# Queries and keys turned by VectorE in 32x32 blocks, in place of TensorE transposes

## What is computed

```python
q = rope(rmsnorm(x @ Wq.T), pos)          # 32 positions x 32 heads x 128
k = rope(rmsnorm(x @ Wk.T), pos)          # 32 positions x  8 heads x 128
v = x @ Wv.T
k_all, v_all = [cached 512 keys, k], [cached 512 values, v]   # pages by block_table
scores = einsum('bqhd,bkhd->bhqk', q, repeat(k_all, 4)) / sqrt(128)
probs  = softmax(where(valid, scores, -1e30))
out    = einsum('bhqk,bkhd->bqhd', probs, repeat(v_all, 4)) @ Wo.T
```

## Time and profile before

| | us |
|---|---|
| median of 3 runs | 3128.94 (3127.9 to 3129.48) |
| the profiled execution | 3137.39 |
| its span | 3135.6 |
| TensorE busy | 3013.1 (96%) |
| VectorE busy | 1545.1 (49%) |
| ScalarE busy | 1285.4 (41%) |
| GpSimd busy | 1467.3 (47%) |

### The profile page before, as it was taken

The page is one execution under the profiler, slowest core; times in us unless marked ns, Lnnn a source line. Parts: engine busy times, 40 slices in busy tenths (PEclk is TensorE's granted clock), DMA queues, the critical chain, the costliest instruction groups (busy, mean ns, idle before and its releaser), DMA issues. The chain is left out here.

```text
span 3135.6 us, 56006 instructions
## 1 busy us (share of the span) xinstructions
PE 3013.1 (96%) x15256; PEld 2016.5 (64%) x15264; DVE 1545.1 (49%) x4043; ACT 1285.4 (41%) x3017; POOL 1467.3 (47%) x1262
## 2 busy tenths in 40 slices
PE   6889999999999999999999999999999998899997
PEld 4566666666666666666666666666666665565664
DVE  4544444444444444444444444444444444576665
ACT  2444444444444444444444444444444442222222
POOL 5465555555555555555555555555555551000000
PEclk9899999999999999999999999999999999899998
DMA  8444443434444444545444444444444344321110
GB/s 302 172 116 120 119 118 118 118 118 118 118 117 118 119 119 119 199 119 172 119 119 119 119 119 119 119 119 119 119 116 118 117 118 135 98 52 44 38 43 14
DMA packets 413898, 368.45 MB, mean 118 GB/s; under 512 B 83415, under 2 KB 347755, under 8 KB 412731
## 3 DMA queue, kind: packets, MB, share of 16 engines
q1 hardware_dynamic: 358490, 186.81, 21.0%
q0 software_dynamic: 48208, 165.16, 17.0%
q10 hardware_dynamic: 7056, 14.46, 1.2%
HBM read 335.13 MB, written 22.71 MB: 114 GB/s over the span
## 5 line engine op out<-in xcount | busy, mean ns | idle before, releaser
L551 DVE CUSTOM_DVE_ANT_0 ps_s<-ps_s,mask 128x544 f32<-128x544 f32 x512 | 374.9, 732 | 912.6 <-PE ps_s L383 738.5
L283 POOL DMA_INDIRECT v_sb<-in_v_rows_w,v_row x504 | 491.9, 976 | 483.5 <-PE ps_oT L408 274.1
L342 PE MATMUL ps_t<-wqkv,xT 128*128 128x512 f32 x1488 | 703.9, 596 | 0.0
L406 PEld LDWEIGHTS ps_oT<-pT,v_sb 128*128 128x128 f32 x4096 | 527.1, 192 | 184.2 <-issue 183.1
L454 ACT ACTIVATE ps_s<-ps_s,nmax 128x544 f32<-128x544 f32 x512 | 352.3, 688 | 596.5 <-DVE nmax L551 546.6
L406 PE MATMUL ps_oT<-pT,v_sb 128*128 128x128 f32 x4096 | 541.4, 275 | 7.8 <-issue 7.8
L366 PE MATMUL ps_t<-wo,oT 128*128 128x512 f32 x1024 | 524.7, 596 | 2.5 <-ACT oT L469 0.9
L382 PE MATMUL ps_s<-k_sb,qT 128*128 128x416 f32 x1024 | 448.5, 520 | 20.3 <-DVE pT_new L567 7.9
L469 ACT ACTIVATE oT<-ps_oT 128x128 f32<-128x128 f32 x512 | 142.3, 278 | 676.1 <-PE ps_oT L408 633.8
L561 DVE TENSOR_SCALAR p_sb<-ps_s,rinv 128x544 f32<-128x544 f32 x512 | 401.4, 784 | 23.5
L391 PEld LDWEIGHTS ps_pT<-ident_sb,p_sb 128*128 128x128 f32 x2048 | 251.5, 141 | 188.7 <-issue 184.3
(11 more groups left out here) (225 smaller groups left out, 3504.1 us busy)
## 6 DMA issues: line engine op xcount, KB each, us to landing
k_sb<-in_kT SPq DMA_DIRECT2D x2048, 64.0 KB
v_sb<-in_v_rows_w,v_row POOLq DMA_INDIRECT x512
v_new<-v_raw SPq DMA_DIRECT2D x128, 64.0 KB, 2.0
wo<-in_wo_w POOLq DMA_DIRECT2D x2, 4096.0 KB, 13.8
y_scratch<-y_sb SPq DMA_DIRECT2D x32, 256.0 KB
xT<-x1T_scratch POOLq DMA_DIRECT2D x31, 256.0 KB, 4.4
wqkv<-in_wqkv_w ACTq DMA_DIRECT2D x6, 1024.0 KB, 25.1
wqkv<-in_wqkv_w POOLq DMA_DIRECT2D x6, 1024.0 KB, 13.2
```

The costliest lines, as they stand in the source:

```text
L283: e.indirect_dma_start(out=v_sb[:, b % 2, c, :], out_offset=None, in_=A["v_rows_w"], in_offset=bass.IndirectOffsetOnAxis(ap=v_row[:, b, c: ...
L342: m = e.matmul(ps_t[bank_of(t)][:, :], xT[:, k, :], wqkv[:, k, 512 * t:512 * t + 512], start=k == 0, stop=k == KC - 1)
L406: e.matmul(ps_oT[:, :], v_sb[:, b % 2, c, h * D:(h + 1) * D], pT[:, u % 2, c, :], start=c == 0, stop=False)
L551: e.tensor_tensor_reduce(out=scores(u), in0=scores(u), in1=mask[:, b % 2, :], scale=-SCALE, scalar=3e38, op0=ALU.add, op1=ALU.min, accum_o ...
```

## The change

TensorE's `turn_q` and ScalarE's `copy_q` are gone from the rounds; the first round's queries and keys are still turned by TensorE, ahead of the rounds. VectorE turns the others, straight from `rot` in SBUF to `qT` and `kT_new` in SBUF, in 32 x 32 blocks: for each sequence b (32 partitions of `rot`) and each quarter j of the 128 numbers, one instruction over the 16 query heads (32 x 512), and one over the four key heads (32 x 4 x 32). That is 32 instructions a round. `qT` is laid out anew, so that what an instruction writes lies together. A table says how many stand in each unit, before and behind the normalisation: units 11 to 15 of the round before, and units 0 to 3 of the round itself, since only the first sequence is needed at once. The waits go by `q_turned`, now counted by instruction. VectorE's loop becomes one over two rounds.

```diff
-    TURN_AT = {8: 0, 9: 1, 10: 2, 11: 3, 12: 4}
+    TURN_AT = {11: (2, 2), 12: (2, 2), 13: (1, 1), 14: (1, 1), 15: (2, 2), 0: (1, 2), 1: (1, 3), 2: (2, 2), 3: (1, 4)}
@@ rotate (GpSimd), before the first write of rot
-            e.wait_ge(W.q_turned, NQT * r)
+            e.wait_ge(W.q_turned, blocks_turned(r - 1, GB - 1) if not (isinstance(r, int) and r == 1) else NQT)
@@ TensorE
-            def turn_q(r, t):
...
-                for h in range(4):
-                    m = e.transpose(ps_t[1][:, h * P:(h + 1) * P], rot[:, 4 * t + h, :], ident[:, :])
-                m.then_inc(q_turned, 1)
@@ score
-                if u == 0:
-                    e.wait_ge(q_copied, NQT * (r + 1))
                 if h == 0:
+                    if first(r):
+                        e.wait_ge(q_copied, NQT)
+                    else:
+                        e.wait_ge(q_turned, blocks_turned(r, b))
@@ ScalarE
-            def copy_q(r, t, i):
...
-                e.activation(to, of, ACT.Copy).then_inc(q_copied, 1)
@@ VectorE
+            def turn(r, i, m):
+                b, j = divmod(m, TURNS)
+                rows, at = slice(S * b, S * b + S), slice(S * (j % 4), S * (j % 4) + S)
+                if m == 0:
+                    e.wait_ge(rope_step, STEPS * (r + 1))
+                    wait(e, scored, UNITS * (r - 1))
+                if j == 4:
+                    e.wait_ge(placed, GB * (r - 1) + b + 1)
+                if j < 4:
+                    e.transpose(qT[at, i, b, :, :], rot[rows, 0:HQH, at]).then_inc(q_turned, 1)
+                else:
+                    e.transpose(kT_new[at, :, rows], rot[rows, HQH:HT, at]).then_inc(q_turned, 1)
...
                     if ahead(r, u, 1) is not None:
                         copy_pT(*ahead(r, u, 1))
+                    turns(r, i, u, 0)
                     if ahead(r, u, 2) is not None:
                         norm(*ahead(r, u, 2))
+                    turns(r, i, u, 1)
...
-            rounds(e, body)
+            pairs(e, body)
```

More of the change, by code:

```diff
@@ L42, with blocks_turned @@
 STEPS, STEPS1 = 15, 6
+TURNS = 2 * (P // S)
+def blocks_turned(r, b):
+    return NQT + TURNS * GB * (r - 1) + TURNS * (b + 1)
 class Shared:
@@ L63, in __init__ @@
         self.w4 = sb("w4", [P, 4, D], F32)
-        self.qT = sb("qT", [P, 2, HKH, GB, REP, S], F32)
+        self.qT = sb("qT", [P, 2, GB, HQH, S], F32)
         self.kT_new = sb("kT_new", [P, HKH, P], F32)
@@ L162, in attention @@
     wo_done, y_copied = sem("wo_done"), sem("y_copied")
-    TURN_AT = {8: 0, 9: 1, 10: 2, 11: 3, 12: 4}
+    TURN_AT = {11: (2, 2), 12: (2, 2), 13: (1, 1), 14: (1, 1), 15: (2, 2), 0: (1, 2), 1: (1, 3), 2: (2, 2), 3: (1, 4)}
+    TURN_NEXT = sum(sum(TURN_AT[u]) for u in range(11, 16))
     OUT_AT = {6: (0, 2), 7: (2, 4), 8: (4, 5), 9: (5, 7), 10: (7, 8), 11: (8, 10), 12: (10, 11), 13: (11, 13), 14: (13, 14), 15: (14, 16)}
@@ L174, in wait @@
             e.wait_ge(s, n)
[L176 to L181, removed]
     def pairs(e, body):
@@ L333, in project @@
                         e.wait_ge(dma_x, 16 * r)
-                        wait(e, q_copied, NQT * r)
+                        e.wait_ge(summed, NQT * r)
                     if t == 1:
@@ L380, in score @@
                 wait(e, p_copied_v, n - 1)
-                q = qT[:, i, h, b, :, :].rearrange("p r s -> p (r s)")
+                q = qT[:, i, b, REP * h:REP * h + REP, :].rearrange("p r s -> p (r s)")
                 e.matmul(ps_s[u % 2][:, FROM:512], q, k_sb[:, b % 2, 0:PAGES1, h, :], start=True, stop=True)
@@ L418, in body @@
                         out_product(r - 1, 1 - i, h0, h0 + 1)
-                    if u in TURN_AT and not last(r):
-                        turn_q(r + 1, TURN_AT[u])
                     if ahead(r, u, 1) is not None:
@@ L475, in copy_y, with place @@
                 e.activation(y_sb[:, :], ps_t[0][:, :], ACT.Copy).then_inc(y_copied, 1)
-            def copy_q(r, t, i):
[L478 to L482, removed]
-                else:
-                    wait(e, placed, GB * r)
-                    to, of = kT_new[:, :, :], ps_t[1][:, :].rearrange("p (h n) -> p h n", h=HKH)
-                e.activation(to, of, ACT.Copy).then_inc(q_copied, 1)
-            def place(r, b):
-                if b == 0:
-                    e.wait_ge(q_copied, NQT * (r + 1))
+            def place(r, b):
+                if first(r):
+                    e.wait_ge(q_copied, NQT)
+                else:
+                    e.wait_ge(q_turned, blocks_turned(r, b))
                 wait(e, scored, UNITS * r + HKH * (b - 1))
@@ L510, in body @@
                         copy_pT(*ahead(r, u, 1))
-                    if u in TURN_AT and not last(r):
-                        copy_q(r + 1, TURN_AT[u], 1 - i)
             exp(0, 0)
@@ L573, in table, with turns, body @@
                 make_tables(e, W, csn[:, 0, :], csn[:, 1, :])
-            def body(r):
+            def turn(r, i, m):
[10 more added lines that the diff above has]
+                    e.transpose(kT_new[at, :, rows], rot[rows, HQH:HT, at]).then_inc(q_turned, 1)
+            def turns(r, i, u, part):
+                if u not in TURN_AT or first(r) and u < 11 or last(r) and u >= 11:
+                    return
+                units = range(11, u) if u >= 11 else range(u)
+                m = (0 if u >= 11 else TURN_NEXT) + sum(sum(TURN_AT[v]) for v in units) + part * TURN_AT[u][0]
+                for n in range(m, m + TURN_AT[u][part]):
+                    turn(r + 1 if u >= 11 else r, 1 - i if u >= 11 else i, n)
+            def body(r, i):
                 for u in range(UNITS):
@@ L896, in copy_q @@
                 if t < HKH:
-                    to, of = W.qT[:, 0, t, :, :, :].rearrange("p b r s -> p r b s"), ps_p[t % 2][:, :].rearrange("p (r b s) -> p r b s", r=REP, b=GB)
+                    to, of = W.qT[:, 0, :, REP * t:REP * t + REP, :].rearrange("p b r s -> p r b s"), ps_p[t % 2][:, :].rearrange("p (r b s) -> p r b s", r=REP, b=GB)
                 else:
```

## The result

| | before | changed |
|---|---|---|
| median of 6 runs, us | 3128.97 (3127.87 to 3129.87) | 3119.32 (3109.05 to 3120.99) |
| profiled execution, us (span) | 3137.4 (3135.6) | 3109.05 (3107.2) |
| ratio of the times | | 0.9961, 95% interval 0.9948 to 0.9975 |

The kernel became faster by 9.7 us. The forecast was 25.7. Of all executions of this case one, of the kernel before with a third buffer, ran at a mean granted clock of 0.87 in place of 0.99 and took 3457.84 us; the ratio in its row leaves it out.

A forecast was written before the change was run, and what follows sets the result against it. TensorE, busy 96% of the span, was taken as the bound; -67.4 for transposes, -7.9 for waits and 31 x 1.6 of new wait gave -25.7 us, from 3128.9 to 3103 us; own range 3085 to 3120, whole range 3062 to 3148.

The forecast's parts named there:

- what TensorE loses: Five groups of transposes leave TensorE's rounds: 2.175 us a round, 67.4 us over 31 rounds.
- what VectorE gains: Turns of 0.73 us (large) and 0.33 us (small) add 17 us a round, bringing VectorE to about 2070 us busy.
- the fullest unit: Unit 11, with four large turns: VectorE's chain makes TensorE's score of unit 13 wait 0.3 us a round.
- the disturbance: Unit 11: TensorE's signals come late during GpSimd's burst of gathers, adding 1.3 us, for 1.6 us of wait a round.
- the burst hangs on GpSimd's rotation: Rotation starts from unit 3's third sum, ahead of removed transposes, so TensorE moves 1.3 to 1.7 us forward against the burst.
- Rival 1: Lateness in unit 11 goes, only 0.3 us of wait a round left: -66 us, 3063 us; chance 0.27.
- Rival 2: Full lateness, 2.6 us a round, and the clock falls after TensorE's holes in 11 rounds: +24 us, 3153 us; chance 0.18.
- Rival 3: Large turn takes two cycles a value, 1.26 us, so unit 11's wait is 3.7 us: +39 us, 3168 us; chance 0.07.
- Rival 4: The wait lands at 2.2 to 2.6 us and eats the gain: within 6 us of 3129; chance 0.13.
- The other edits: GpSimd's wait for the last turn, waits on the turn count and VectorE's loop over two rounds: all counted at nothing.

The follow-up runs named there:

- third buffer: Third buffer for gathered values, the fourth sequence's gathers issued at round start, attention output of 8 heads: on changed kernel 3063.95 us, on kernel before 3115.25 us.
- two gathers away: Two of the fourth sequence's four gathers in own memory, issued at round start, single mask: on changed kernel 3069.16 us, on kernel before 3120.29 us.
- the still later gathers: Kernel before with an unused GpSimd power of 128x12 numbers between rotation and gathers: 3144.36 us, ratio 1.0034.
- the small turns: Changed kernel with VectorE turns of one head in place of 16 or 4 inside the loops: 3109.26 us; with the third buffer too, 3057.55 us.

## Why the prediction was right and wrong

**Right: what TensorE loses.** Units 8 to 11 are shorter by 0.44 us each once nothing else is late, and unit 12 by 0.35 (two gathers away against the kernel before with the same: 2298.0 against 2355.9 us for 30 rounds, 57.9 of the 65.3 us of the term).

**Right: what VectorE gains.** A large turn takes 0.702 us (0.73 taken), a small one 0.302 (0.33), VectorE is busy 2097 us (2070). Two large ones last 1.42 us, so neighbours do not overlap. The Trainium skill, "VectorE: DVE Perf Modes", section "Two Vector instructions with no wait between them", has the rule for it: an instruction that starts in another group of 32 partitions than the last one waits until the earlier ones are done. The rows agree. (The prediction's 215 to 250 ns for one of the four copies are 215 to 283 in the trace; nothing hangs on it.)

**Right, but hidden: the fullest unit.** The chain gives 0.3 us of wait at the score of unit 13. With the gathers out of the way a round shows 0.26 us of idle time there in the profile, and unit 12 is 0.39 us shorter without the large turns. In the changed kernel itself the gathers' wait, which stands just before that score, covers it: VectorE's copy at L376 is waited for 5.5 us in all (7.9 before), 1.4 of them there.

**Wrong: the disturbance.** The forecast added 1.3 us for signals that reach VectorE late, and took GpSimd's burst for their whole cause. In the changed kernel the masking of unit 11 starts 0.2 us after its scores in all 30 rounds, though these end 1.4 us (1.1 to 1.9) behind the burst's start, so within it; the copy is late by more than 1 us in one round. Two things that the change also brings take the lateness of unit 11 away from the kernel before, each alone: VectorE's loop over two rounds with the burst in place, and a burst that comes 1.6 us later against TensorE (the still later gathers; in the changed kernel TensorE comes 1.3 us earlier). Which of them did it in the changed kernel isn't shown. The loop was counted at nothing, and by itself it takes the 9.0 us of waits out of unit 11. 1.3 us a round, 40 us in all, stood in the sum for something that did not come.

**The step that failed** is the sentence that the burst hangs on GpSimd's rotation, "so TensorE moves 1.3 to 1.7 us forward against it". It was used to place the late signals, and the question behind it was not asked: what is in the burst, and who waits for it. TensorE moves 2.2 us forward against gathers that it needs in unit 12, and they had 0.9 us of cover. The sum has no term for them. By the profile of before alone: 2.18 us of transposes and 0.3 of waits at unit 11 (9.0 in 30 rounds) that go, less 0.93 of cover, are 1.54 us a round. Measured are 1.33 us before the weighing in the first profile and 1.62 in the second, and 0.2 us behind it in both. In 30 rounds, by the first: -65.3 for the transposes, -8.6 for the waits at unit 11, +45.6 in unit 12 (40 of them before the weighing), -1.7 elsewhere: -30.0, from 2369.7 to 2339.7 us. By the second it is -18.8. That the sum of the forecast came out near this (-25.7) is chance: it had 1.6 us a round of wait in the right neighbourhood for another reason. By the medians the change brought 9.7.

**What stays open** is the rest to the medians. The second profile of the changed kernel, which took its median time, is 17.9 us under the profiled execution of before, and 8.4 of these are that execution's distance from its own median. No profile of before at its median is there, so where these 8 us lie isn't known.

**The rivals.** Rival 1 had the lateness go and 3063 us; the lateness went, and 3063.95 us is what the kernel takes without the gathers' wait, which no rival had. That the two numbers agree is chance too, since the buffer also takes 13 us from the first round and from round 15. Rival 2 had the clock fall in 11 rounds. Behind the hole of 2.51 us in the 6th round it stayed at the 2.4 GHz level (1.00); behind that of 2.76 in the 23rd a part of 4 us was at the 1.2 GHz level (mean 0.66). Stretches behind each of the two (us; busy us of PE, PEld, DVE, ACT, POOL; clock, DMA):

```profile
1984.40:1988.40 4.00, 4.00 (x16) 2.67 (x17) 1.46 (x5) 0.48 (x2) 2.41 (x4) 0.66 0.19 66
656.40:660.40 4.00, 4.00 (x23) 2.92 (x24) 2.14 (x6) 1.13 (x4) 2.24 (x4) 1.00 0.21 68
```

Rival 3 is out by the 0.702 us. Rival 4, a wait of 2.2 to 2.6 us that eats the gain to within 6 us of 3129, asks for less than was gained, and has another cause. The measured 3119 us stands at the slow end of the forecast's own 3085 to 3120.

**The other edits.** GpSimd's wait for the last turn and VectorE's for the rotation cost nothing seen (1.1 us in all before the turns). VectorE's loop over two rounds cost no time on the kernel before, as said. In the changed kernel TensorE waits 3.9 us in unit 15 of five odd rounds (3 to 11) for VectorE's normalisation (`p_sb L542` in the row of L376), which it did not before; why isn't shown.

## What to carry to other kernels

When the bounding engine gets faster, list every transfer and every other engine's result that it consumes later in the round and that does not move with it, and read the cover of each; a cover of 0.9 us shows nowhere as idle time, so look for another instruction that waits for the same transfer and compare the two starts. A burst that disturbs is also a burst that somebody waits for. An edit that is counted at nothing, like the form of a loop, can take waits out of one unit and put them into another while the time stands still, so compare unit by unit. And where a wait is relieved, the next one can be just behind: here 0.3 us of VectorE behind 1.5 us of gathers.

## What the runs showed of the hardware

- A transposition in blocks of 32 by 32 on VectorE takes 0.702 us for 32x512 numbers of 4 bytes, 0.302 for 32x128, and 0.202 for 32x32 (the small turns), so 1.04 ns for each column more, beside some 0.17 us.
- From the end of an arithmetic instruction on GpSimd, which is waited for, to the indirect DMA behind it there are 0.89 us (0.17 at 547.10 of the kernel before, where it isn't waited for); an addition put between them starts 0.08 us after it, and the DMA then 0.16 us after the addition.
- While GpSimd issues a burst of gathers, signals of TensorE can reach VectorE late: 1.8 to 3.2 us in unit 11 of the kernel before, 2.0 to 2.1 in unit 13 with the third buffer. Not every burst does it. With another form of VectorE's loop, and nothing else changed, it was 0.2 to 0.57 us at the same place. Why wasn't found.
- Four gathers landed 1.11 us later when their issue came 1.64 us later.
